# A merge stage with its inverted sums spread by a product, its normalized rows made by ScalarE, and a buffer for every batch

## What is computed

```python
ctx = jnp.einsum('bhqk,bkhd->bqhd', attn, v).reshape(b, t, EMB)
return ctx @ wo + bo          # layer 0; layer 1 returns its ctx without a projection
...
x = x + attention(h, wq, wk, wv, wo, bo)
h = layernorm(x, ln2_scale, ln2_shift)
```

## Time and profile before

| what | us |
|---|---|
| median of 3 runs | 2215.17 (2200.15 to 2220.67) |
| the profiled execution, its own time | 2213.47 |
| its span in the trace | 2212.0 |
| stage m: first load 619.67 to the first load of stage e 693.81 | 74.14 |
| stage r and what is left of stage d: 1110 to 2075.09 | 965.09 |
| stage n: first load 2075.09 to the first load of stage f 2133.62 | 58.53 |

### The profile page before, as it was taken

How to read it: one execution, slowest core, us unless ns; L and a number is a source line. 1 busy time by engine, 2 the same in 40 slices (tenths; PEclk the granted TensorE clock), 3 DMA queues, 4 the chain that set the end, 5 groups by cost and what they waited for, 6 DMA issues and landing times. The chain is left out here.

```text
span 2212.0 us, 53944 instructions
## 1 busy us (share of the span) xinstructions
PE 1545.4 (70%) x18859; PEld 988.0 (45%) x19047; DVE 1324.4 (60%) x3180; ACT 1029.8 (47%) x1964; POOL 345.8 (16%) x633
## 2 busy tenths in 40 slices
PE   5532447777722999997525888887878787888447
PEld 2211224444422666664212655555545555555323
DVE  4774277667445676664421766575756575677546
ACT  4332316666700323321414776575757566676203
POOL 2232325555432000000210000000000000000013
PEclk8766659999955999998865999798989898999759
DMA  1114722222146122121888999999999999999442
GB/s 38 43 39 142 235 56 63 62 54 70 29 127 218 51 77 81 52 105 35 245 217 302 334 363 361 351 344 333 344 341 346 336 343 344 338 341 349 126 134 57
DMA packets 194998, 432.92 MB, mean 196 GB/s; under 512 B 37776, under 2 KB 86576, under 8 KB 185360
## 3 DMA queue, kind: packets, MB, share of 16 engines
q1 hardware_dynamic: 171376, 248.53, 36.9%
q10 hardware_dynamic: 12672, 152.05, 16.5%
q0 software_dynamic: 10720, 29.11, 5.1%
HBM read 225.80 MB, written 203.55 MB: 194 GB/s over the span
## 5 line engine op out<-in xcount | busy, mean ns | idle before, releaser
L2083 DVE CUSTOM_DVE_ANT_0 r_shifted<-r_ps_ac,r_shifted 128x512 f32<-128x512 f32 x512 | 352.1, 688 | 319.9 <-PE r_ps_ac L1960 137.1
L2049 ACT ACTIVATE r_probs<-r_ps_keys 128x512 f32<-128x512 f32 x512 | 309.6, 605 | 265.9 <-PE r_ps_keys L1967 233.6
L1967 PE MATMUL r_ps_keys<-r_ident,r_shifted 128*128 128x128 f32 x2048 | 333.0, 288 | 69.6 <-DMA r_v<-v 36.6
L2028 ACT ACTIVATE r_wide<-r_ps_wide 128x512 f32<-128x512 f32 (+1 forms) x576 | 329.7, 591 | 79.4 <-PE r_ps_wide L1951 78.8
L1967 PEld LDWEIGHTS r_ps_keys<-r_ident,r_shifted 128*128 128x128 f32 x2048 | 273.4, 149 | 50.5 <-issue 9.8
L1951 PE MATMUL r_ps_wide<-r_r,r_qv 48*32 48x64 bf16 (+12 forms) x6144 | 239.0, 256 | 62.3 <-issue 49.4
L2091 DVE TENSOR_SCALAR r_shifted<-r_shifted,r_mx 128x512 f32<-128x512 f32 x512 | 249.2, 487 | 18.3
L860 ACT ACTIVATE c_probs<-c_ps_keys 128x512 f32<-128x512 f32 (+1 forms) x384 | 174.7, 530 | 149.6 <-PE c_ps_keys L786 149.4
L1951 PEld LDWEIGHTS r_ps_wide<-r_r,r_qv 48*32 48x32 bf16 x6144 | 103.7, 95 | 165.1 <-issue 163.8
L1427 ACT ACTIVATE e_silu<-e_ps_a 128x1024 f32<-128x1024 f32 x64 | 65.7, 1027 | 216.1 <-PE e_ps_a L1360 216.1
L923 DVE TENSOR_REDUCE c_mx_off<-c_ps_rows 128x2 f32<-128x768 f32 (+2 forms) x192 | 120.8, 686 | 63.7 <-PE c_ps_rows L757 63.7
(11 more groups left out here) (201 smaller groups left out, 2138.0 us busy)
## 6 DMA issues: line engine op xcount, KB each, us to landing
skew<-r_wide ACTq DMA_DIRECT2D x64, 2224.0 KB, 11.9
r_shifted<-skew SPq DMA_DIRECT2D x64, 2048.0 KB, 17.0
e_weight_all<-weights SPq DMA_DIRECT2D x8, 2048.0 KB, 7.6
c_qk<-qk_stacks POOLq DMA_DIRECT2D x64, 192.0 KB, 3.7
stack<-d_part SPq DMA_DIRECT2D x96, 128.0 KB, 2.7
qk_stacks<-b_part SPq DMA_DIRECT2D x48, 128.0 KB, 3.4
qk_stacks<-b_part POOLq DMA_DIRECT2D x48, 128.0 KB, 3.7
stack<-d_part POOLq DMA_DIRECT2D x48, 128.0 KB, 4.0
```

Of the source, the lines that this page charges most:

```text
L1967: last = pe.transpose(ps_keys[u % 2][:, j * P:(j + 1) * P], shifted[:, s, u, j * P:(j + 1) * P], ident[:, :])
L2028: act.activation(wide[:, s, c, lo:hi], ps_wide[bk % BANKS][:, 0:hi - lo], ACT.Copy).then_inc(wide_sb, 1)
L2049: act.activation(probs[:, h % 2, :, b * P:(b + 1) * P], ps_keys[u % 2][:, :].rearrange("p (j i) -> p j i", j=NT), ACT.Exp, scale=SCALE).th ...
L2083: dve.tensor_tensor_reduce(out=shifted[:, s, u, :], in0=ps_ac[u % 2][:, :], in1=shifted[:, s, u, :], scale=1.0, scalar=LOWEST, op0=ALU.add ...
```

## The change

Both runs of `phase_merge` are rewritten, everything else stays:

- **Inverted sums.** The round trip through the DRAM tensor `inverted` goes, and the tensor with it. VectorE makes `heads`, the identity with each column repeated eight times (L1122 of the new file, 128x1024), inverts `den` in place (L1124), and TensorE multiplies: one fp32 product of 512 columns per batch (`invert`, L1095) writes the inverted sums, repeated over the rows of each head, to PSUM (`ps_inv`, three buffers), where `divide` reads them (L1119).
- **Normalized rows.** z = xa * rstd + minus is made by ScalarE, four activations Identity of 128 columns per batch, with scale and bias read per row (L1057). GpSimd computes minus = (0 - mean) * rstd in two small operations (L1078, L1085) around `root`.
- **base** moves from GpSimd to VectorE (L1143), behind the statistics; xb stays on GpSimd, three batches ahead (L1065).
- **Buffers and loads.** Every tensor has eight buffers, one per batch. SP issues den and the eight loads of num at once and later the stores; ScalarE issues ident, bo, w and the eight loads of x at once. No loop is left; products have three PSUM buffers.
- **New waits.** VectorE's statistics of batch n + 1 wait for `minus_ready` of batch n (one buffer of mean), GpSimd's root of batch n + 1 waits for `z_ready` of batch n (one buffer of rstd), z waits for `minus_ready` of its own batch.

```diff
-def phase_merge(nc, sems, ctx_in, x_in, w_in, b_in, base_out, z_out, inverted, name):
+def phase_merge(nc, sems, ctx_in, x_in, w_in, b_in, ident_in, base_out, z_out, name):
...
+        SETS = 3
-        num = sb("num", [P, 2, L])
+        ident = sb("ident", [P, P])
+        heads = sb("heads", [P, P, DH])
-        den_inv = sb("den_inv", [P, L])
-        inv = sb("inv", [P, 2, L])
+        num = sb("num", [P, NB, L])
+        x = sb("x", [P, NB, NT, P])
+        xb = sb("xb", [P, NB, NT, P])
...
+        minus = sb("minus", [P, NB, NT])
+        zeros = sb("zeros", [P, NT])
...
+        ps = [ctx.enter_context(nc.psum_tensor(f"{name}_ps{i}", [P, L], F32)) for i in range(SETS)]
+        ps_inv = [ctx.enter_context(nc.psum_tensor(f"{name}_ps_inv{i}", [P, L], F32)) for i in range(SETS)]
...
         @block.sync
         def _(sp):
             sp.dma_start(den[:, :], ctx_in.rearrange("n h r t -> (n h) r t")[:, DH, :]).then_inc(den_loaded, 16)
...
+            for n in range(NB):
+                sums = ctx_in.rearrange("(b g) h r t -> b g h r t", g=NG)[n].rearrange("g h r t -> (g h) r t")
+                sp.dma_start(num[:, n, :], sums[:, 0:DH, :]).then_inc(num_loaded[n], 16)
+            for n in range(NB):
+                if base_out is not None:
+                    sp.wait_ge(base_ready, n + 1)
+                    sp.dma_start(base_out[n], base[:, n, :, :]).then_inc(stored, 16)
+                sp.wait_ge(z_ready, n + 1)
+                sp.dma_start(z_out[n], z[:, n, :, :]).then_inc(stored, 16)
+            sp.wait_ge(stored, 16 * NB * (1 + (base_out is not None)))
...
         @block.scalar
         def _(act):
...
+            act.dma_start(ident[:, :], ident_in).then_inc(ident_loaded, 16)
+            if b_in is not None:
+                act.dma_start(bo[:, :], row_on_all(b_in)).then_inc(bo_loaded, 16)
+            act.dma_start(x[:, 0, :, :], x_in[0]).then_inc(x_loaded[0], 16)
+            act.dma_start(w[:, :], w_in).then_inc(w_loaded, 16)
+            for n in range(1, NB):
+                act.dma_start(x[:, n, :, :], x_in[n]).then_inc(x_loaded[n], 16)
+            for n in range(NB):
+                act.wait_ge(xa_ready, n + 1)
+                act.wait_ge(minus_ready, n + 1)
+                for t in range(NT):
+                    last = act.activation(z[:, n, t, :], xa[:, n, t, :], ACT.Identity, bias=minus[:, n, t:t + 1],
+                                          scale=norm.rstd[:, t:t + 1])
+                last.then_inc(z_ready, 1)
...
         @block.gpsimd
         def _(pool):
...
+            AHEAD = 3
+            pool.memset(zeros[:, :], 0.0).then_inc(zeros_set, 1)
+            pool.wait_ge(zeros_set, 1)
+            norm.constants(pool)
+            if b_in is not None:
+                pool.wait_ge(bo_loaded, 16)
+                for n in range(AHEAD):
+                    add_bias(n)
+            for n in range(NB):
+                pool.wait_ge(norm.var_ready, n + 1)
+                pool.tensor_tensor(minus[:, n, :], zeros[:, :], norm.mv[:, :, 0], ALU.subtract)\
+                    .then_inc(minus_mean, 1)
+                if n >= 1:
+                    pool.wait_ge(z_ready, n)
                 norm.root(pool, n + 1)
-                if base_out is not None:
...
-                    pool.tensor_tensor(base[:, s, :, :], xa[:, s, :, :], x[:, s, :, :], ALU.add)\
-                        .then_inc(base_ready, 1)
...
+                pool.wait_ge(minus_mean, n + 1)
+                pool.wait_ge(norm.rstd_ready, n + 1)
+                pool.tensor_tensor(minus[:, n, :], minus[:, n, :], norm.rstd[:, :], ALU.mult)\
+                    .then_inc(minus_ready, 1)
+                if b_in is not None and n + AHEAD < NB:
+                    add_bias(n + AHEAD)
 
         @block.tensor
         def _(pe):
...
+            def invert(n):
+                if n >= SETS:
+                    pe.wait_ge(cT_ready, n - SETS + 1)
+                pe.matmul(ps_inv[n % SETS][:, :], heads[:, H * n:H * (n + 1), :].rearrange("p h d -> p (h d)"),
+                          den[:, :], start=True, stop=True).then_inc(inv_ps, 1)
+
+            pe.wait_ge(heads_set, 1)
+            pe.wait_ge(den_inverted, 1)
+            for n in range(2):
+                invert(n)
+            pe.wait_ge(w_loaded, 16)
+            for n in range(NB):
+                if n + 2 < NB:
+                    invert(n + 2)
+                pe.wait_ge(cT_ready, n + 1)
+                if n >= SETS:
+                    pe.wait_ge(xa_ready, n - SETS + 1)
+                for t in range(NT):
+                    last = pe.matmul(ps[n % SETS][:, t * P:(t + 1) * P], cT[:, n, t * P:(t + 1) * P], w[:, :],
+                                     start=True, stop=True)
+                last.then_inc(a_ps, 1)
 
         @block.vector
         def _(dve):
...
+            def divide(n):
+                dve.wait_ge(num_loaded[n], 16)
+                dve.wait_ge(inv_ps, n + 1)
+                dve.tensor_tensor(cT[:, n, :], num[:, n, :], ps_inv[n % SETS][:, :], ALU.mult).then_inc(cT_ready, 1)
+
+            dve.wait_ge(ident_loaded, 16)
+            dve.tensor_copy(heads[:, :, :], ident[:, :].unsqueeze(2).broadcast_to([P, P, DH])).then_inc(heads_set, 1)
+            dve.wait_ge(den_loaded, 16)
+            dve.reciprocal(den[:, :], den[:, :]).then_inc(den_inverted, 1)
+            divide(0)
+            for n in range(NB):
+                if n + 1 < NB:
+                    divide(n + 1)
...
-                dve.wait_ge(stored[s], n_out * (it + 1))
+                    dve.wait_ge(x_loaded[n], 16)
...
-                dve.tensor_tensor(xa[:, s, :, :], ps[s][:, :].rearrange("p (t d) -> p t d", t=NT),
+                dve.tensor_tensor(xa[:, n, :, :], ps[n % SETS][:, :].rearrange("p (t d) -> p t d", t=NT),
+                                  src[:, n, :, :], ALU.add).then_inc(xa_ready, 1)
+                dve.wait_ge(xa_ready, n + 1)
+                if n >= 1:
+                    dve.wait_ge(minus_ready, n)
+                norm.moments(dve, xa[:, n, :, :], n + 1)
+                if base_out is not None:
+                    dve.wait_ge(x_loaded[n], 16)
+                    dve.tensor_tensor(base[:, n, :, :], xa[:, n, :, :], x[:, n, :, :], ALU.add)\
+                        .then_inc(base_ready, 1)
...
-    inverted = [dram(f"inverted{i}", (NB, H, 1, L)) for i in range(2)]
...
-    phase_merge(nc, sems, sums[0], x1, wo, bo, base, z2, inverted[0], "m")
+    phase_merge(nc, sems, sums[0], x1, wo, bo, ident, base, z2, "m")
...
-    phase_merge(nc, sems, sums[1], x2, ident, None, None, x3, inverted[1], "n")
+    phase_merge(nc, sems, sums[1], x2, ident, None, ident, None, x3, "n")
```

More of the change, by code:

```diff
@@ L1016, in phase_merge @@
         base_ready = sem("base_ready")
+        minus_mean = sem("minus_mean")
+        minus_ready = sem("minus_ready")
         z_ready = sem("z_ready")
-        stored = [sem("stored0"), sem("stored1")]
-        n_const = 16 + 16 * (b_in is not None)
-        n_out = 16 + 16 * (base_out is not None)
+        stored = sem("stored")
         block = sems.block(ctx)
-        def load(eng, n, s):
-            sums = ctx_in.rearrange("(b g) h r t -> b g h r t", g=NG)[n].rearrange("g h r t -> (g h) r t")
-            eng.dma_start(num[:, s, :], sums[:, 0:DH, :]).then_inc(loaded[s], 16)
-            eng.dma_start(inv[:, s, :], inverted[n].broadcast_to([H, DH, L])).then_inc(loaded[s], 16)
-        def load_x(eng, n, s):
-            eng.dma_start(x[:, s, :, :], x_in[n]).then_inc(x_loaded[s], 16)
-        def steps(step, eng):
-            with eng.Fori(0, NB // 2 - 1) as it:
-                for s in range(2):
-                    step(it, s, True)
-            for s in range(2):
-                step(NB // 2 - 1, s, s == 0)
         @block.sync
@@ L1042, in _ @@
             sp.dma_start(den[:, :], ctx_in.rearrange("n h r t -> (n h) r t")[:, DH, :]).then_inc(den_loaded, 16)
-            sp.dma_start(w[:, :], w_in).then_inc(consts, 16)
-            if b_in is not None:
-                sp.dma_start(bo[:, :], row_on_all(b_in)).then_inc(consts, 16)
-            for s in range(2):
-                load_x(sp, s, s)
-                sp.sem_inc(stored[s], n_out)
-            sp.wait_ge(den_inverted, 1)
-            sp.dma_start(inverted.rearrange("b h o t -> (b h) (o t)"), den_inv[:, :]).then_inc(inv_stored, 16)
@@ L1051, in _ @@
-            sp.wait_ge(inv_stored, 16)
-            for s in range(2):
-                load(sp, s, s)
-            with sp.Fori(0, NB // 2) as it:
-                for s in range(2):
-                    n = 2 * it + s
-                    sp.wait_ge(cT_ready, n + 1)
-                    load(sp, (n + 2) % NB, s)
-                    if base_out is None:
-                        sp.wait_ge(xa_ready, n + 3)
-                    else:
-                        sp.wait_ge(base_ready, n + 1)
-                    load_x(sp, (n + 2) % NB, s)
@@ L1066, in _ @@
-            for s in range(2):
```

(30 more changed lines are left out.)

55 lines of the change are left out of this document (12 added, 43 removed).

## The result

Over 20 executions of each kernel the changed one has a median of 2201.36 us (2192.96 to 2214.17), the kernel before 2214.46 us (2200.15 to 2220.67): the ratio is 0.9944, with an interval of 0.9928 to 0.9961. That is 13 us or 0.6% less, where 36 us were forecast, and it lies above the top of the range, 2195. The profiled execution took 2203.24 us (span 2201.5).

What follows compares the result with a forecast made beforehand. A chain of waits through VectorE, with no engine full, was taken to bound the merge stages. Start, seven shorter turns and end gave -23.8 us (m) and -12.3 (n): 2213.5 - 36.1 = 2177 us, range 2160 to 2195.

Steps and rivals of the forecast that it cites:

- the sum: Whole kernel: stage m -23.8 us and stage n -12.3, in all -36.1, from 2213.5 to 2177.
- Start, -1.15 per stage: Begin of each merge stage: first xa at 634.0 instead of 635.15, the DRAM round trip mostly replaced by cold products.
- Turns, 3.85 and 3.35: Time per batch in us, stage m and stage n, forecast from 6.99 and 5.08 before.
- The ring: Each batch: statistics, GpSimd's subtraction, sum, root and multiplication, then next statistics; 3.32 us, 0.5 more in stage m from base.
- ScalarE's z, 1.58: Four activations per batch in both merge stages take 1.58 us (bounds 1.1 and 2.7), narrowly hidden.
- TensorE warm: Merge stages: full clock from the first batches on, about 2.0 us of products per batch instead of 3.9, hidden.
- TensorE's clock at 1.0 from the third batch on: Sign expected in the merge stages' profile if TensorE leaves the half clock it had before.
- the TensorE rival: Merge stages: TensorE stays at half clock and becomes the bound, turns of 3.92 us, 2184 in all; chance 0.08.
- that of z: Merge stages: ScalarE's z takes 2.7 us and closes a ring of 4.44, 2191 in all; chance 0.09.
- the burst of loads: Start of both merge stages: loads share the engines evenly, first cT 6 us later, 2189 in all; chance 0.07.
- End: Last xa to stage end: stage m +0.6 - 1.3 us, stage n +0.9.
- stage r pays: Stage r slows as its scratch tensors move 0.5 MB in memory; at 7% 2245 us; stage r changed, chance 0.10.

Runs made afterwards that it cites:

- the five profiles at 43.05: Changed kernel twice, changed with unused `inverted` tensors, kernel before plus 117 TensorE instructions, kernel before with new stage m alone: 2201.36, 2205.36, 2198.83, 2241.55, 2214.93 us.
- the two at 42.59: The kernel before, unedited, 2214.46 us; and the kernel before with the new merge in stage n alone, 2202.32 us.
- the one at 43.59: Changed kernel with 139 more TensorE instructions (waits already met) ahead of stage r's products: 2190.13 us, ratio 0.9874.

## Why the prediction was wrong

Inside the two stages the mechanism of the change was read rightly, with small misses; the sum was wrong because it stopped at their edges.

*Start, -1.15 per stage.* It was -2.0 in stage m and -2.5 in stage n (first xa 13.50 and 13.14 us behind the stage's begin). The copy took the 0.69 of the earlier trace rows, not 1.2, but what it waits for landed later than assumed, 3.3 us behind the begin of either stage instead of 2.74, so the inversion began where it was forecast (3.9 us behind the begin, as in the sum). The gain is TensorE's, which was slow only until the first projection: three spread products (two passes each, x6) took 5.21 us, 1.74 each, the four of the projection behind them 1.05 instead of 2.07:

```profile
630.25 0.69 DVE L1122 COPY m_heads<-m_ident 128x1024 f32<-128x1024 f32 x1 [30.84 <-DMA m_ident<-in_ident_dram]
630.86 3.35 DVE L1124 RECIPROCAL m_den<-m_den 128x512 f32<-128x512 f32 x1
634.35 5.21 PE L1095 MATMUL m_ps_inv<-m_den,m_heads 128*128 128x512 f32 x6 [12.34 <-DVE m_den L1124]
639.40 1.05 PE L1110 MATMUL m_ps<-m_w,m_cT 128*128 128x128 f32 x8
640.49 0.69 DVE L1135 TENSOR_TENSOR m_xa<-m_ps,m_xb 128x512 f32<-128x512 f32 x1 [1.59 <-PE m_ps L1110]
```

*Turns, 3.85 and 3.35.* Measured 3.73 and 3.45 (statistics of the first and the eighth batch, 641.22 to 667.30 and 2092.26 to 2116.41, by seven). One turn of stage m, VectorE and GpSimd:

```profile
644.97 0.87 DVE L105 BATCH_NORM_STATS2 m_norm_stats<-m_xa 128x6 f32<-128x128 f32 x4 [0.58 <-POOL m_minus L1085]
...
646.28 0.66 DVE L1143 TENSOR_TENSOR m_base<-m_xa,m_x 128x512 f32<-128x512 f32 x1
646.44 0.55 POOL L1078 TENSOR_TENSOR m_minus<-m_zeros,m_norm_mv 128x4 f32<-128x4 f32 x1 [0.35 <-DVE m_norm_mv L111]
...
646.95 0.20 POOL L116 TENSOR_TENSOR m_norm_var_eps<-m_norm_mv,m_norm_consts 128x4 f32<-128x4 f32 x1
647.23 1.02 POOL L119 TENSOR_TENSOR m_norm_rstd<-m_norm_var_eps,m_norm_consts 128x4 f32<-128x4 f32 x1
...
648.39 0.20 POOL L1085 TENSOR_TENSOR m_minus<-m_minus,m_norm_rstd 128x4 f32<-128x4 f32 x1
...
648.69 0.87 DVE L105 BATCH_NORM_STATS2 m_norm_stats<-m_xa 128x6 f32<-128x128 f32 x4 [0.56 <-POOL m_minus L1085]
```

The ring closes as forecast, and the statistics wait 0.56 for it. The subtraction is held by base, as forecast: it takes 0.55 us instead of the 0.20 of stage n, where there is no base, and ends with base. But the turn is only 0.28 longer than stage n's, where 0.5 was put into the sum. It was so in all eight batches (552 to 554 ns). By the rule of the Trainium skill that the prediction drew on (SBUF - State Buffer, section Who interferes with whom), the second of the two to come is held until the first is over; the trace agrees.

*ScalarE's z, 1.58.* 1.65, hidden. *TensorE warm.* The products of a batch take 1.05 to 1.16 us in the first six batches of either stage, against 2.07 in the earlier trace rows; granted clock in stage m 1.00 from 640 to 656. The sign "TensorE's clock at 1.0 from the third batch on" holds only up to there: behind the last spread product (652.3) TensorE has nothing but the four products of a batch, the clock is 0.50 from 660 on, and the products of the last two batches take 2.07 again. It costs nothing, the statistics still follow each other in 3.7 us. So neither the TensorE rival nor that of z came, and the burst of loads did not delay the first cT. *End.* Stage m -1.2 (forecast -0.7), stage n +0.9 (+0.9). All together -26.0 and -13.0 where the sum had -23.8 and -12.3.

**The step that failed** is the sum: "In all -36.1: 2213.5 - 36.1 = 2177". It holds only if nothing else in the program moves, and it took that for granted for some 2080 us of work whose source is unchanged. Its own sign fired: stage r, to stay within 0.5%, took 2.5% longer (930.1 to 953.0). With the loop's begin moved by 28 instructions, to 43.16, the changed kernel takes 2172.3 us, 5 below the forecast, and the stages were 3 better than their sum; so the rest of the working was sound. The missing term is the loop of stage r in its code's new place: 696.1 us on average over the five profiles at 43.05, against 667.9 over the two at 42.59 and the one at 43.59, the same place within a piece: +28, 21 of them second stops.

The rival "stage r pays" had the right stage and the wrong cause: it looked at addresses of data, which the run with the tensors kept showed to be worth nothing (loop 702.5 us with them, 698.2 and 694.6 without), not at where the instructions lie. What could have told was in the trace of before: branches of 3.6 to 7.1 us on TensorE beside 0.06 on VectorE, 27.4 us of "issue" at the loop's head, and queue q8 bringing the program in by 16 KB. With the 117 instructions that stage m adds on TensorE these make a rival of its own, though not yet its sign: where a piece ends in the loop is known only from the experiments. The section of the Trainium skill on fetching (Runtime: NRT & Kernel Launch, section Instruction fetch mechanics) calls the crossing from one block to the next mostly hidden; by that alone the place of a loop within its blocks would be worth nothing, and 22.3 us of second stops in the changed kernel say otherwise for a crossing soon behind a jump.

## What to carry to other kernels

Where an engine's program is long, a gain in one stage is not a gain of the whole until the later loops have been looked at: take the stages apart by their begins in both traces, and look for "issue" waits behind a loop's jump and for long branch rows. When an unrelated stage moves, put a few instructions that do nothing ahead of its loop, in the kernel before as well as in the changed one; if the time follows, compare the two at one place, or write the loop out on the engine with the long program. Here 28 such instructions were worth 29 us and the loop written out 36, beside the 39 of the merge stages. Too many of them cost time themselves, as the rows of 192 and 232 did at the start of stage r.

## What the runs showed that was not expected

A jump back in stage r's loop cost TensorE 3.4 to 7.6 us (5.6 on average in the kernel before) and VectorE 0.06, while in the same program TensorE jumped back over 617 instructions in 0.23 us. A second stop followed when little of the piece was left behind the target: 3.4 to 5.7 us with some 18 instructions left (five kernels), 3.1 to 3.7 with 43, 1.1 to 2.3 with 82, and with some 136 one of 1.3 us in fifteen jumps (in the kernel with the new stage n alone), counted to an end at 43.12. 117 instructions that do nothing made a kernel of 2214 us 1.0% slower.

Open are three things. A piece takes 1.1 us on its queue, yet in the changed kernel it is 2.4 to 3.8 us from the begin of the branch to the start of the target's piece and 2.7 to 3.3 more to the first product: what these wait for is not shown. From how many instructions on a loop is fetched anew at each turn lies, by these kernels, between 617 and 2312. And why 192 or 232 added instructions cost the start of stage r 10 to 20 us more than 28 do is not known.
